# Moving four tile products of an attention kernel from the end of one key block to the ends of four

## What is computed

```python
xn = _layernorm(x)
q = (xn @ Wq.T).reshape(n, s, 16, 16)
k = jnp.repeat((xn @ Wk.T).reshape(n, s, 8, 16), 2, axis=2)
v = jnp.repeat((xn @ Wv.T).reshape(n, s, 8, 16), 2, axis=2)
energy = jnp.einsum('nqhd,nkhd->nhqk', q, k) + alibi_bias
attn = softmax(energy / 4, axis=-1)
att = jnp.einsum('nhqk,nkhd->nqhd', attn, v).reshape(n, s, 256) @ Wo.T + bo
x_scale = max(max(abs(xn)), 1e-6) / 127          # one for each token
x_q = clip(round(xn / x_scale), -128, 127)
lin = (x_q @ weight_q.T) * x_scale * weight_scale + bias
out = x + att + lin
```

## Time and profile before

| | |
|---|---|
| median of three runs | 1541.24 us |
| the profiled execution | 1540.39 us |
| its span, first to last instruction | 1538.6 us |
| PE busy | 1487.8 us (97%) |
| DVE busy | 1395.7 us (91%) |
| ACT busy | 1185.2 us (77%) |
| POOL busy | 1059.4 us (69%) |
| mean granted TensorE clock | 0.996 |
| DMA queue, share of 16 engines | 33.9% |

### The profile page before, as it was taken

How to read it: one execution, slowest core, us unless ns; L and a number is a source line. 1 busy time by engine, 2 the same in 40 slices (tenths; PEclk the granted TensorE clock), 3 DMA queues, 4 the chain that set the end, 5 groups by cost and what they waited for, 6 DMA issues and landing times.

```text
span 1538.6 us, 41766 instructions
## 1 busy us (share of the span) xinstructions
PE 1487.8 (97%) x15956; PEld 577.5 (38%) x15956; DVE 1395.7 (91%) x1704; ACT 1185.2 (77%) x2337; POOL 1059.4 (69%) x1607
## 2 busy tenths in 40 slices
PE   6889999999999999999999999999999999999998
PEld 6323333333333333333343333333333333333333
DVE  6899999999999999999999999999999889999981
ACT  4477877777877777887777877777877778888885
POOL 6467887777888887877777877777877764333332
PEclk9899999999999999999999999999999999999999
DMA  6622323333333333333333333333333322222212
GB/s 174 150 73 78 90 79 102 81 102 95 100 84 102 96 103 96 94 90 102 96 102 91 105 85 98 99 100 98 100 83 95 90 77 72 66 57 67 63 45 63
DMA packets 196136, 140.14 MB, mean 91 GB/s; under 512 B 106656, under 2 KB 164832, under 8 KB 195936
## 3 DMA queue, kind: packets, MB, share of 16 engines
q1 hardware_dynamic: 195936, 137.47, 33.9%
HBM read 80.61 MB, written 35.62 MB: 76 GB/s over the span
## 4 chain that ended last, share of the span: by engine, by line
PE 52%; DVE 35%; issue 9%; SPq 2%; POOL 1%; DMA 1%; ACT 0%; POOLq 0%; DVEq 0%
DVE row_max L1003 32%; PE ps_ring L1289 16%; PE ps_pv L1365 14%; PE ps_row L1306 11%; PE ps_ring L1401 4%; PE ps_ring L1421 3%; PE ps_ring L1404 1%; DVE pv_turned L1043 1%; PE ps_ring L1415 1%; PE ps_row L1393 1%; SPq L440 1%; SPq L464 0%; SPq L468 0%; DVE stats L911 0%; DMA q<-neg_max_t 0%
## 5 line engine op out<-in xcount | busy, mean ns | idle before, releaser
L1003 DVE TENSOR_REDUCE row_max<-ps_row 128x1 f32<-128x1024 f32 x1024 | 1199.6, 1213 | 86.3 <-PE ps_row L1308 79.9
L1180 ACT ACTIVATE probs<-ps_ring 128x512 f32<-128x512 f32 x2048 | 1082.3, 601 | 222.3 <-PE ps_ring L1289 219.8
L1289 PE MATMUL ps_ring<-q,k 122*32 122x512 bf16 x8192 | 633.6, 382 | 4.8 <-DMA q<-neg_max_t 4.0
L758 POOL TENSOR_TENSOR probs<-probs,near 128x256 f32<-128x256 f32 x512 | 374.0, 730 | 317.6 <-ACT probs L1180 311.4
L1365 PE MATMUL ps_pv<-probs,v_unit 128*32 128x512 f32 x4096 | 530.4, 593 | 0.0
L1289 PEld LDWEIGHTS ps_ring<-q,k 122*32 122x32 bf16 x8192 | 215.2, 95 | 499.9 <-ACT probs L1180 320.7
L1306 PE MATMUL ps_row<-k,q 64*128 64x512 bf16 x1000 | 345.7, 385 | 25.7 <-DVE row_max L1003 10.1
L1308 PE MATMUL ps_row<-k_again,q_again 64*128 64x512 bf16 x1000 | 345.6, 385 | 0.0
L1306 PEld LDWEIGHTS ps_row<-k,q 64*128 64x128 bf16 x1000 | 90.1, 93 | 338.5 <-issue 210.2
L1365 PEld LDWEIGHTS ps_pv<-probs,v_unit 128*32 128x32 f32 x4096 | 124.6, 109 | 50.5 <-issue 7.0
L1308 PEld LDWEIGHTS ps_row<-k_again,q_again 64*128 64x128 bf16 x1000 | 89.9, 92 | 0.0
(11 more groups left out here) (85 smaller groups left out, 976.6 us busy)
## 6 DMA issues: line engine op xcount, KB each, us to landing
parts_dram<-parts SPq DMA_DIRECT2D x58, 288.0 KB, 3.7
q_again<-q SPq DMA_DIRECT2D x63, 256.0 KB, 3.3
token_b<-token_dram SPq DMA_DIRECT2D x51, 256.0 KB, 4.4
q<-parts_dram SPq DMA_DIRECT2D x128, 96.0 KB
k<-parts_dram SPq DMA_DIRECT2D x256, 32.0 KB
q<-parts_dram SPq DMA_DIRECT2D x128, 64.0 KB
att_dram<-att_unit SPq DMA_DIRECT2D x126, 64.0 KB
att_t<-att_dram SPq DMA_DIRECT2D x56, 128.0 KB, 2.9
```

Of the source, the lines that this page charges most:

```text
L758: pool.tensor_tensor(here, here, near[:, u % KV_HEADS, :].rearrange("p (e n) -> p e n", e=GROUP), ALU.mult).then_inc(weighted, 1)
L1003: dve.tensor_reduce(row_max[:, par, e, qb:qb + 1], ps_row[qb % 2][:, :], AX_X, ALU.max, negate=True).then_inc(row_max_found, 1)
L1180: act.activation(probs[:, c % PBUFS, e, h * HALF:(h + 1) * HALF], ring_bank(u, c, e, h), ACT.Exp, scale=SCALE).then_inc(ring_freed, 1)
L1289: mm = pe.matmul(to[at, :], weights[:, at], moving, start=start, stop=stop)
```

## The change

- PE and ACT: an odd unit's tile products stand one at the end of a block: queries, keys and values of the first tile at block 1 and of the second at block 3, outputs of the first at block 5 and of the second at block 7 (`QKV_AT`, `OUTPUTS_AT`, `pieces_of`). `ring_places` numbers the banks in the new order.
- DVE, from unit 2 on: the first tile is normalised at block 3 and the second at block 5; statistics of the first are taken at block 3, of the second at block 7.
- POOL: the second tile's high part is split at block 3 and its middle part at block 4; the first tile's linear layer is weighed at block 6.
- SP: `store_token` and `store_parts` of the second tile stand behind `place_max` of the next unit. At the start, `place_max(0, 0)` stands ahead of `load_again(1, 1)` and the loads of `wo` and `wo_last`.

No instruction of computation is added or taken away. The core of the diff:

```diff
+QKV_AT, OUTPUTS_AT = (1, 3), (5, 7)
...
+def pieces_of(u, c):
+    f = flags_of(u)
+    if c in QKV_AT:
+        return [("qkv", t) for t in f["made"][QKV_AT.index(c):][:1]]
+    if c in OUTPUTS_AT:
+        return [("outputs", t) for t in (f["proj"] or f["made"])[OUTPUTS_AT.index(c):][:1]]
+    return []
...
             items = [(u, c, e, h) for e in range(GROUP) for h in range(2)]
-            if c == 1:
-                items += [(u, "outputs", t % PAIR) for t in f["proj"] or f["made"]]
-                items += [(u, "qkv", t % PAIR) for t in f["made"]]
+            items += [(u, what, t % PAIR) for what, t in pieces_of(u, c)]
...
             load_set(2, 2)
+            place_max(0, 0)
             load_again(1, 1)
...
             store_token(PREP_AHEAD)
-            place_max(0, 0)
...
-                for t in f["normed"]:
+                for t in f["normed"][:1]:
                     store_token(t)
-                for t in f["made"]:
+                for t in f["made"][:1]:
                     store_parts(t, t % 2)
...
                 if f["prev"] and u % PAIR == 0:
                     store_att(u - 1)
+                for t in f["normed"][1:]:
+                    store_token(t)
+                for t in f["made"][1:]:
+                    store_parts(t, t % 2)
...
+                normed_at = {3: 0, 5: 1} if u >= PAIR else {1: 0, 3: 1}
+                stats_at = {3: 0, 7: 1} if u >= PAIR else {1: 0, 3: 1}
...
-                    if c == 1:
-                        for t in f["proj"] or f["made"]:
+                    for what, t in pieces_of(u, c):
+                        if what == "qkv":
+                            qkv_whole(u, t)
+                        else:
                             outputs(u, f, t % PAIR)
-                        for t in f["made"]:
-                            qkv_whole(u, t)
```

More of the change, by code:

```diff
@@ L139, in ring_places @@
     for u in range(UNITS):
-        f = flags_of(u)
         for c in range(BLOCKS):
             items = [(u, c, e, h) for e in range(GROUP) for h in range(2)]
-            if c == 1:
-                items += [(u, "outputs", t % PAIR) for t in f["proj"] or f["made"]]
-                items += [(u, "qkv", t % PAIR) for t in f["made"]]
+            items += [(u, what, t % PAIR) for what, t in pieces_of(u, c)]
             for item in items:
@@ L855, in unit @@
                             split_middle(made)
-                    if c == 2:
-                        for made in f["made"][1:]:
-                            split_high(made)
                     if c == 3 and not f["last"]:
@@ L862, in unit @@
                         for made in f["made"][1:]:
+                            split_high(made)
+                    if c == 4:
+                        for made in f["made"][1:]:
                             split_middle(made)
-                    if c == 4:
-                        for made in f["made"][:1]:
-                            weigh_linear(made)
                     if c == 4 and f["turned"]:
@@ L879, in unit @@
                         keep_rounded(t)
+                    if c == 6:
+                        for made in f["made"][:1]:
+                            weigh_linear(made)
                     if c == 7:
@@ L1073, in unit @@
                 at_sums, at_norm = (5, BLOCKS) if apart else (3, 3)
-                made = 1 if u < PAIR else PAIR
-                def here(c):
-                    return slice(0, made) if c == 1 else slice(made, PAIR)
+                normed_at = {3: 0, 5: 1} if u >= PAIR else {1: 0, 3: 1}
+                stats_at = {3: 0, 7: 1} if u >= PAIR else {1: 0, 3: 1}
                 for c in range(BLOCKS):
@@ L1094, in unit @@
                             turn_back(u - 1)
-                    if c in (1, 3):
-                        for t in f["normed"][here(c)]:
+                    if c in normed_at:
+                        for t in f["normed"][normed_at[c]:][:1]:
                             normalise(t, t % 2)
@@ L1099, in unit @@
                             find_scale(t, t % 2)
-                        for t in f["stats"][here(c)]:
+                    if c in stats_at:
+                        for t in f["stats"][stats_at[c]:][:1]:
                             wait(dve, x_loaded, 16 * (t - X_AHEAD + 1))
@@ L1212, in unit @@
                             exps(u, c, e, h)
-                    if c == 1:
-                        for t in f["proj"] or f["made"]:
+                    for what, t in pieces_of(u, c):
+                        if what == "qkv":
+                            keep_qkv_whole(u, t)
+                        else:
                             keep_outputs(u, f, t % PAIR)
-                        for t in f["made"]:
-                            keep_qkv_whole(u, t)
             for i in range(2, FIRST_PARTS):
```

## The result

Four runs of the changed kernel have a median of 1569.24 us (1568.3 to 1570.55), four of the kernel before 1541.16 us. The ratio is 1.0182, 95% interval 1.0167 to 1.0198: slower by 1.8%, and 2.2 us above the predicted 1567.

What follows compares the result with a forecast made beforehand. The bound was taken to be the loop in which PE and DVE pass work to each other, no single engine. Terms +17.2, +10.4, +2.1 and -4.0 sum to 25.7 on 1540.39; with 0.85 for the median, 1567 us, range 1550 to 1576.

Steps and rivals of the forecast that it cites:

- The loop: PE and DVE between row products: PE's additions at odd block ends paid in full, DVE's hidden within PE's plus 0.28 us.
- Two signs: DVE was to idle before the first reductions of blocks 2, 4, 6 and 0, nowhere longer than about 1 us.
- Units 9 to 51: 22 full odd units: four separate products take 6.74 in place of 5.96 us, 0.78 more each, +17.2 us.
- The price per visit: Each separate tile product on PE pays 0.20 us for array shape, plus 0.09 if it begins with an fp32 load.
- Units 53 to 61: Five odd units with projections alone: PE's burst and DVE's work at block 1 are parted, 2.07 us each, +10.4 us.
- Units 1 to 7: Early odd units: 0.55 us more in three units and 0.4 in unit 1, +2.1 us.
- The start: First maxima moved ahead let PE begin key products sooner: -4.0 us, between -0.9 and -6.
- The clock's share: At the start, a shorter PE stand may let the next stretch run at full clock: 0 to 2.3 us, taken as 1.
- the two cases of the text: `wo` at the start: PE starts at 72.7 (0.9 us gained) or 69.9 (3.7 gained); 3 was taken.
- no wait for banks: Rival: the toll at tile products is a bank wait and goes away, 1541 us, no change; chance 0.06.
- products did not vanish behind DVE: Rival: spread products hide behind DVE's own work in odd units, 1517 us, faster; chance 0.07.
- the maxima did not hold up later units: Rival: maxima come late on SP, so about 24 units after odd ones start 1 us late, 1591 us; chance 0.05.

Runs made afterwards that it cites:

- the run with even blocks: The changed kernel with the four products at the ends of blocks 0, 2, 4 and 6, DVE's work left in place: 1595.70 us.
- both strip runs: Tile products made in four strips of 32 columns, in the changed kernel (1540.95 us) and in the burst of the kernel before (1533.01 us).
- two places: The changed kernel with queries, keys and values of both tiles at block 1 and outputs of both at block 5: 1554.82 us.
- fp32 first: The changed kernel with the fp32 projection ahead of the linear layer in outputs: 1573.35 us.
- the earlier scaling: The changed kernel with POOL's scaling of the turned tile moved from block 4 to block 2: 1568.23 us.
- strips: The changed kernel with each tile product made in four strips of 32 columns: 1540.95 us.
- late units: As a run: the changed kernel with both projections of odd units 53 to 63 back at block 1: 1558.10 us.
- the burst in strips: The kernel before with its burst of four tile products made in strips of 32 columns, nothing moved: 1533.01 us.
- the start alone: The kernel before with only the first maxima placed ahead of the copies and weights: 1535.48 us.

## Why the prediction was right

- *The size.* The sum missed the profiled pair by 4.4 us (25.7 for 30.1): 2.8 in the units and 1.6 at the start, and all but one of the terms came out too low. That the medians miss by only 2.2 is in part luck of the executions.
- *The loop* held at each place: steps of 4.25, 4.26, 3.47 and 3.47 for 4.24 and 3.45, and even units untouched. Two signs failed in part: DVE doesn't idle before block 6 of a full odd unit, since the slowed normalisation ends just in time, and in late units it idles for 1.45, over the 1 us named. The rule's words "odd block" are too narrow, as the run with even blocks shows: without work of DVE beside it, a product costs the same at an even one.
- *Units 9 to 51*: 0.84 for 0.78. The price per visit and its two parts are confirmed by four runs: shape (both strip runs), number (two places), fp32 load (fp32 first). By the rule that hides the load the sum would be 5.4 us lower, further from the measured time. The Trainium skill, TensorEngine Tiling (Array Packing), section Key Properties, on the drain at a change of mode, agrees with the trace: 0.09 to 0.10 on the way in (0.31 or 0.32 to the first product, in fp32 and in bf16, in place of 0.22), and about as much on the way out (the projection takes 0.96 up to the key product behind, 344.55 to 345.51, and 0.87 within the burst). The load's 0.09 comes on top, inside the product.
- *Units 53 to 61*: 1.99 for 2.07, one unit 2.13. The parting of two works that covered each other is shown by the run that put them together again.
- *Units 1 to 7*: 3.75 for 2.1, the term most mis-sized. That POOL slows the normalisation at block 5 was missing: 0.41 in each of units 3, 5 and 7, as the earlier scaling shows. That is 1.2 of the 1.65 missed; unit 1, with 0.66 in place of 0.4, is another 0.26, and the rest stays open.
- *Unit 63*: 0.25 for 0. ACT does not pace it, as the prediction says: in the kernel before ACT is busy for 13.97 of its 19.0 us and PE for 18.45, and with the burst in strips it takes 18.74.
- *The start*: -2.4 for -4.0 in the profiled pair. The clock's share (1) was not there in that execution, and `wo` landed at about 71.0, between the two cases of the text. Five other profiled executions with the same start and odd blocks (strips, two places, fp32 first, late units, scaling) reached the first `turn_pv` at 95.35 to 99.23, the burst in strips with the old one at 103.82. The stand ahead of the first key product, ended by `wo` in all five, goes from 0.36 to 2.24 us; only behind the two shortest (0.36 and 0.47) was the granted clock 1.00, so the clock's share came in two of five. One pair sizes the term only to a few microseconds; by medians the start alone is worth 5.3, more than the 4.0 predicted.
- *The rivals*: no wait for banks, though idle time before weight loads rose (32.7 at L1412, 16.6 at the burst); products did not vanish behind DVE; the maxima did not hold up later units (even units take 20.47 as before). At the start `wo` did take the maxima's place, but with a shorter stand.

## What to carry to other kernels

Where two engines pass work through two buffers, find the loop first, and price an addition by the place in it where it stands and by what the other engine does there; work of two engines that covers one another must be moved together or not at all. Splitting a burst costs a toll for each visit: give the piece the shape of the work around it before splitting it, and count visits, not instructions. Even without the toll the split gained nothing here: in strips it takes 1540.95 us, though its start gains, and the burst in strips with its old start 1533.01. Idle time before a weight load tells little about delay: look at the distance from matmul to matmul.

## What the runs showed that was not expected

- A product is no slower in strips: 64 matmuls in strips take 1.74 us, 16 with the whole array 1.79. In the kernel before, strips gain 0.6% by themselves.
- A DVE normalisation beside a POOL multiplication takes 0.79 to 0.91 us in place of 0.41. The Trainium skill, SBUF — State Buffer, section SBUF: two separate sides, has DVE, in some of its modes, and GpSimd share a port pair, held for a whole instruction while the other is blocked. The trace agrees in kind: POOL's row begins first, at 344.61, DVE's at 344.83, and that ends 0.2 us after POOL's next instruction has begun at 345.42. Whether this normalisation runs in such a mode no run shows.
- After a stand of 1.61 us at the start PE ran the next 4.5 us at a granted clock of 0.50, as it did after 3.99; after 1.42, in the run of the start alone, the next 4.0 us at a mean of 0.57. In the run with the late units at block 1, which has the same start, the stand was 0.36 and the window behind it had 1.00:

```profile
68.44 0.62 PE L1302 MATMUL ps_ring<-q,k 122*32 122x512 bf16 x8 [0.36 <-DMA wo<-wo_t]
...
68.40:73.00 4.60, 3.96 (x44) 1.09 (x44) 4.53 (x5) 3.73 (x8) 1.61 (x3) 1.00 0.54 137
```
